# Last chunk's keys ahead of the last value projections, shifts stored by head group, rotary angles of self-attention computed in stage one, opening reordered

## The reference

```python
q = x @ W_q + b_q                      # x layer-normed, 512 rows
kv = y @ W_kv + b_kv                   # y: 8192 context rows
q, k = apply_rope(q, cos_q, sin_q), apply_rope(k, cos_k, sin_k)   # angle = position * frequency
attn = softmax(q @ k.T / sqrt(32))     # 16 heads of 32
x = x + (attn @ v) @ W_o + b_o
theta = pos * INV_FREQ * exp(log_scale)       # self-attention: one angle per head, row and pair
q, k = _rotate(q, cos(theta), sin(theta)), _rotate(k, cos(theta), sin(theta))
```

## Time and profile before

| | us |
|---|---|
| runs, median of 3 | 1724.97 (1720.51 to 1726.48) |
| profiled execution | 1718.63 |
| its span | 1717.3 |
| PE busy | 1598.6 (93%) |
| DVE busy | 1179.8 (69%) |
| ACT busy | 1080.9 (63%) |
| Pool busy | 720.7 (42%) |
| mean granted TensorE clock | 0.955 of full speed |

### The profile page before, as it was taken

How to read it: one execution, slowest core, us unless ns; L and a number is a source line. 1 busy time by engine, 2 the same in 40 slices (tenths; PEclk the granted TensorE clock), 3 DMA queues, 4 the chain that set the end, 5 groups by cost and what they waited for, 6 DMA issues and landing times.

```text
span 1717.3 us, 25439 instructions
## 1 busy us (share of the span) xinstructions
PE 1598.6 (93%) x9532; PEld 973.7 (57%) x9532; DVE 1179.8 (69%) x2759; ACT 1080.9 (63%) x1269; POOL 720.7 (42%) x385
## 2 busy tenths in 40 slices
PE   6599999999999779999999999999888879999998
PEld 4466666666666443434443444444655467888886
DVE  5567777777877759999988988998674452222222
...
GB/s 143 123 184 176 132 136 167 141 136 156 152 136 133 126 178 98 123 101 120 123 123 122 111 121 115 123 123 74 83 27 56 2 3 176 124 123 123 125 128 54
DMA packets 87339, 202.61 MB, mean 118 GB/s; under 512 B 8828, under 2 KB 9084, under 8 KB 84400
## 3 DMA queue, kind: packets, MB, share of 16 engines
...
## 4 chain that ended last, share of the span: by engine, by line
PE 77%; DVE 9%; issue 6%; ACT 5%; DMA 1%; POOL 1%; SPq 1%; DVEq 0%; ACTq 0%; POOLq 0%
PE PS L114 41%; PE PS L637 12%; PE PS L669 11%; PE PS L411 7%; DVE acc L660 2%; ACT P L643 2%; PE PS L679 1%; PE PS L828 1%; DVE rc L940 1%; PE PS L825 1%; DMA y<-in_wq 1%; DVE rel L424 1%; PE PS L153 1%; DVE rec L614 1%; PE PS L910 1%
## 5 line engine op out<-in xcount | busy, mean ns | idle before, releaser
L643 ACT ACTIVATE P<-PS 128x1024 f32<-128x1024 f32 x512 | 481.9, 1037 | 99.0 <-PE PS L637 81.7
L660 DVE TENSOR_TENSOR acc<-acc,P 128x2048 f32<-128x2048 f32 x216 | 507.7, 2414 | 34.3 <-ACT P L643 34.2
L424 DVE CUSTOM_DVE_ANT_0 rel<-PS,rel 128x256 f32<-128x256 f32 x1024 | 363.2, 420 | 135.8 <-PE PS L411 131.4
L417 ACT ACTIVATE rel<-PS 128x1024 f32<-128x1024 f32 x256 | 263.3, 1029 | 113.1 <-PE PS L411 109.2
L669 PE MATMUL PS<-P,qe 128*32 128x512 f32 x2048 | 258.8, 604 | 0.7 <-ACT on L674 0.7
L108 POOL TENSOR_TENSOR w3l<-qk,w3h 128x2048 fp32r<-128x2048 f32 x2 | 9.1, 4562 | 482.7 <-ACT w3h L105 482.7
L108 POOL TENSOR_TENSOR El<-We,Eh 128x1536 fp32r<-128x1536 f32 x36 | 126.0, 3501 | 166.3 <-ACT Eh L105 166.2
L114 PE MATMUL PS<-Wh,R 128*128 128x512 f32 x512 | 188.3, 424 | 0.0
L114 PE MATMUL PS<-R,Eh 128*128 128x512 f32 x576 | 182.2, 397 | 3.0 <-POOL El L108 3.0
L114 PE MATMUL PS<-R,Wh 128*128 128x512 f32 x512 | 167.3, 408 | 10.0 <-ACT kr L510 9.0
L411 PE MATMUL PS<-khd,qh 32*128 32x256 f32 x2048 | 134.0, 336 | 29.6 <-POOL khd L384 10.7
...
## 6 DMA issues: line engine op xcount, KB each, us to landing
khd<-kscr SPq DMA_DIRECT2D x129, 256.0 KB, 4.0
...
qe<-vscr SPq DMA_DIRECT2D x64, 256.0 KB, 4.7
kl<-kscr SPq DMA_DIRECT2D x63, 256.0 KB, 3.9
```

What stands on the lines that cost most here:

```text
L417: return AC.sig(nc.scalar.activation(rel[i][:, :, :, :], PS[:, 2 * b:2 * b + 2, :].rearrange("p j (t n) -> p j t n", t=2), ACT.Relu))
L424: m = DV.sig(nc.vector.tensor_tensor_reduce(out=rel[i][:, j, t, :], in0=PS[:, 2 * b + j, t * 256:(t + 1) * 256], in1=rel[i][:, j, t, :], s ...
L643: expm[s, pr] = spfree[b] = AC.sig(nc.scalar.activation(P[s % 4][:, 2 * pr:2 * pr + 2, :], PS[:, 2 * b:2 * b + 2, :], ACT.Exp, scale=SCALE))
L660: accm[s] = DV.sig(nc.vector.tensor_tensor(a[:, :, :], a[:, :, :], P[s % 4][:, :, :], ALU.add))
```

## The change

- The opening loads the first context chunk and the key weights first and warms PE with 40 instead of 22 transposes. The angles of the table come first on DVE, then the split of chunk 0; three key units run before the query input is transposed and a fourth before the queries are projected. The queries are swapped by a DVE shuffle and rotated group by group in slots of units 4 to 9 (`rotate_query`, `query_high`, `query_low`). The first chunk's ropes run on DVE. The low halves of `wq`, `wv` and chunk 0 are DVE's.
- Pairs start at slot 120 and follow every 11 slots until they are back in the old places at pair 48; from pair 112 on they follow every 10.
- In the last two chunks the order is keys of 14, keys of 15, values of 14, values of 15. The queries are loaded right behind the last unit.
- Shifts are reduced, transposed, copied and written to row 96 for each head group by itself (`maxima_out`, `maxima_rows`), and stage two waits for the group that it needs. `hot` puts a matmul in each third slot behind the last unit. The three rows of ones are set behind the barrier.
- The angles of self-attention are computed on DVE in 28 steps in units 29 to 56 (`angle_step`), their sines and cosines on ACT in units 64 to 75 (`wave_step`). `ks` and `vo` get tiles of their own, and `cs2` first serves as `ang` and `nn`.

```diff
+        t_ex = AC.sig(nc.scalar.activation(ex[:, :], cst[:, 4:8], ACT.Exp))
...
-        ks, vo = cs2[:, 0, :, :], [cs2[:, 1, :, :]]
+        ks, vo = sbx("ks", [128, 4, 512]), [sbx("vo", [128, 4, 512])]
         cs = [sbx(f"cs{i}", [128, 2, 512]) for i in range(2)]
-        ang = sbx("ang", [128, 1536])
-        nn = sbx("nn", [128, 1536])
+        ang, nn = [cs2[:, i, :, :].rearrange("p a b -> p (a b)")[:, 0:1536] for i in range(2)]
...
-        wq, wk, wv, xn, qsw = y[0], vo[0], kr[1], ks, ks
+        wq, wk, wv, xn, qsw = ks, vo[0], kr[1], qe, kr[1]
...
+        t_y0 = load_input(0)
         t_wk = lane("l_wk").dma(SP, wk[:, :, :], wkv_[:, :, 0:512])
+        t_x = l_a.dma(SP, X[:, :, :], A["x"].rearrange("o (t p) d -> p (o t) d", p=128))
+        t_wq = l_w.dma(SP, wq[:, :, :], A["wq"].rearrange("(k p) n -> p k n", p=128))
...
+        warm(40, 7)
...
+        t_y0s = split(y[0][:, :, :], yh[0][:, :, :], yl[0][:, :, :], t_y0)
+        SP.wait(t_y0s)
+        t_y1 = load_input(1)
+        t_wks = split(wk[:, :, :], Wh[:, :, 0:512], Wl[:, :, 0:512], t_wk)
...
+        t_cs = AC.sig(nc.scalar.mul(nn[:, 0:1024], sinv[:, 0:1024], -1.0))
+        SP.wait(t_cs)
+        for hf in range(2):
+            for s in range(2):
                 for t, src in ((0, cosv), (1, nn if s == 0 else sinv)):
-                    t_cscr = l_t.dma(SP, cscr[:, hf, s, :, t, :], src[:, hf * 512:(hf + 1) * 512])
+                    t_cscr = l_t[hf].dma(SP, cscr[:, hf, s, :, t, :], src[:, hf * 512:(hf + 1) * 512])
...
+        t_wqs = split(wq[:, :, :], wqh[:, :, :], wql[:, :, :], t_wq)
...
+        def rotate_query(g):
+            z, x_ = qsw[:, g, :], qe[:, g, :]
+            DV.wait(ev[g], ev_sign, t_wvs)
+            m_ = DV.sig(nc.vector.stream_shuffle(z, x_, halves))
+            DV.wait(m_)
+            a = DV.sig(nc.vector.tensor_tensor(x_, x_, cosq, ALU.mult))
+            b_ = DV.sig(nc.vector.tensor_tensor(z, z, sinq, ALU.mult))
+            DV.wait(a, b_)
+            qrot[g] = DV.sig(nc.vector.tensor_tensor(x_, x_, z, ALU.add))
+        def query_high(g):
+            AC.wait(qrot[g])
+            qhm[g] = AC.sig(nc.scalar.copy(qh[:, g, :], qe[:, g, :]))
+        def query_low():
+            DV.wait(qhm[3], qrot[3])
+            t_ql = DV.sig(nc.vector.tensor_tensor(ql[:, :, :], qe[:, :, :], qh[:, :, :].bitcast(F32), ALU.subtract))
+            SP.wait(qhm[3], t_ql)
+            qout.append(write_parts(SP, l_q, (qh, ql)))
...
+            DV.wait(kev[c][g], t_wqs, ropes.get((c - 1, g)))
             m = DV.sig(nc.vector.stream_shuffle(z, x, halves))
-            PL.wait(m, csm[c])
-            a = PL.sig(nc.gpsimd.tensor_tensor(x, x, ct[:, 0, :], ALU.mult))
-            b_ = PL.sig(nc.gpsimd.tensor_tensor(z, z, ct[:, 1, :], ALU.mult))
-            PL.wait(a, b_)
-            ropes[c, g] = PL.sig(nc.gpsimd.tensor_tensor(x, x, z, ALU.add))
-            PL.wait(ropes[c, g], max_last.get(c - 2))
-            khd_m[c, g] = PL.sig(nc.gpsimd.tensor_tensor(khd[c % 2][:, g, 512:768], x[:, 0:256], x[:, 256:512], ALU.subtract))
+            E = PL if c else DV
+            E.wait(m, csm[c])
+            a = E.sig(E.e.tensor_tensor(x, x, ct[:, 0, :], ALU.mult))
+            b_ = E.sig(E.e.tensor_tensor(z, z, ct[:, 1, :], ALU.mult))
+            E.wait(a, b_)
+            ropes[c, g] = E.sig(E.e.tensor_tensor(x, x, z, ALU.add))
+            E.wait(ropes[c, g], max_last.get(c - 2))
+            khd_m[c, g] = E.sig(E.e.tensor_tensor(khd[c % 2][:, g, 512:768], x[:, 0:256], x[:, 256:512], ALU.subtract))
...
+        angle_steps, trig, wave = [], [None] * 4, {}
+        def load_positions():
+            SP.wait(t_cscr, list(qrot.values()))
+            wave["pos"] = l_a.dma(SP, cosv[:, 0:512], A["c_pos"].to_broadcast([128, 512]))
+        def first_angle():
+            DV.wait(wave["pos"], t_ex)
+            wave["pr"] = DV.sig(nc.vector.tensor_scalar(cosv[:, 512:1024], cosv[:, 0:512], cst[:, 2:3], None, ALU.mult))
+        def angle_step(g, k):
+            a, n_ = cs2[:, 1, g, :], cs2[:, 0, g, :]
+            DV.wait(trig[g] if k else wave["pr"])
+            if k == 0:
+                ins = nc.vector.tensor_scalar(a, cosv[:, 512:1024], ex[:, g:g + 1], None, ALU.mult)
+            elif k == 1:
+                ins = nc.vector.tensor_scalar(n_, a, INV2PI, MAGIC, ALU.mult, ALU.add)
+            elif k == 2:
+                ins = nc.vector.tensor_scalar(n_, n_, MAGIC, None, ALU.subtract)
+            elif k < 6:
+                ins = nc.vector.scalar_tensor_tensor(a, n_, -(P2A, P2B, P2C)[k - 3], a, ALU.mult, ALU.add)
+            else:
+                ins = nc.vector.tensor_scalar(a, a, 3.1415925, -3.1415925, ALU.min, ALU.max)
+            trig[g] = DV.sig(ins)
+        def wave_step(g, k):
+            a, n_ = cs2[:, 1, g, :], cs2[:, 0, g, :]
+            AC.wait(wave[g, k - 1] if k else trig[g])
+            if k == 0:
+                ins = nc.scalar.activation(n_, a, ACT.Abs)
+            elif k == 1:
+                ins = nc.scalar.activation(a, a, ACT.Sin, scale=cst[:, 20:21])
+            else:
+                ins = nc.scalar.activation(n_, n_, ACT.Sin, scale=-1.0, bias=hpi[:, 0:1])
+            wave[g, k] = AC.sig(ins)
...
+        def hot(n):
+            for _ in range(n):
+                nc.tensor.matmul(PS[:, 7, :], qh[:, 0, 0:128], qh[:, 0, :], start=True, stop=True)
...
+        def maxima_out(g):
+            DV.wait(DV.last())
+            t_nmg[g] = DV.sig(nc.vector.tensor_reduce(nm[:, g:16:4, :], mpart[:, g:16:4, :, :], AX, ALU.max, negate=True))
+        def maxima_rows(g):
+            PE.wait(t_nmg[g], bank[1][0], nm_free.get(g - 1))
+            for qt in range(4):
+                ins = nc.tensor.transpose(PS[0:4, 6, qt * 128:(qt + 1) * 128], nm[:, g:16:4, qt], ident[:, :])
+            AC.wait(PE.sig(ins))
+            nm_free[g] = m = AC.sig(nc.scalar.copy(nmT[32 * g:32 * g + 4, :], PS[0:4, 6, :]))
+            SP.wait(m, k_use[NCH - 1], k_use[NCH - 2])
+            for j, x_ in enumerate((Wh, Wl)):
+                t_qmx[g] = l_nm[g].dma(SP, x_[96:97, :, :].rearrange("p a b -> p (a b)")
+                                       .rearrange("p (h g n) -> p h g n", h=2, g=4)[:, :, g, :],
+                                       nmT[32 * g + 2 * j:32 * g + 2 * j + 2, :])
...
+        def first_key(c):
+            return 8 * c - (4 if c == NCH - 1 else 0)
+        for g, u in enumerate((4, 5, 7, 9)):
+            at(u, 0, rope, 0, g)
+            at(u, 1, rotate_query, g)
+            at(u + 1, 4, key_high, 0, g)
+            at(u + 1, 8, query_high, g)
+        at(12, 0, query_low)
+        at(26, 0, load_positions)
+        at(28, 0, first_angle)
+        for g in range(4):
+            for k in range(7):
+                at(29 + 7 * g + k, 0, angle_step, g, k)
+            for k in range(3):
+                at(64 + 3 * g + k, 11, wave_step, g, k)
         for c in range(NCH):
             if c + 1 < NCH:
+                d = 0 if c else 4
                 for k, (u, m) in enumerate(((0, 9), (1, 4), (1, 9), (2, 4))):
-                    at(8 * c + u, m, y_high, c + 1, k)
-                at(8 * c + 2, 4, y_low, c + 1)
+                    at(8 * c + u + d, m - (7 if c == 14 else 0), y_high, c + 1, k)
+                at(8 * c + 2 + d, 4 - (7 if c == 14 else 0), y_low, c + 1)
             for g in range(4):
-                at(8 * c + g + 1, 10, rope, c, g)
-                at(8 * c + g + 5, 4, key_high, c, g)
-            at(8 * c + 8, 5, key_low, c)
+                if c:
+                    at(first_key(c) + g + 1, 10, rope, c, g)
+                    at(first_key(c) + g + 5, 4, key_high, c, g)
+            at(first_key(c) + (8 if c else 11), 5, key_low, c)
             for i in range(8):
-                at(8 * c + 6 + i, 2, maxima_1, c, i)
-                at(8 * c + 6 + i, 7, maxima_2, c, i)
-        for c in range(NCH):
-            kev[c] = []
-            for u in range(8):
+                n = 8 * c + i
+                m = max(12 * (6 + n), 12 * 10 + 11 * n) - 2 * max(0, n - 8 * 14)
+                at_slot(m + 2, maxima_1, c, i)
+                at_slot(m + 7, maxima_2, c, i)
+                if c == NCH - 1 and i % 2:
+                    at_slot(m + 9, maxima_out, i // 2)
+                    at_slot(m + 17, maxima_rows, i // 2)
+        order = [(c, u) for c in range(NCH - 2) for u in range(8)]
+        order += [(NCH - 2 + v % 2, 4 * h + u) for h in range(2) for v in range(2) for u in range(4)]
+        for c, u in order:
+            kev.setdefault(c, [])
+            if True:
+                if c == 0 and u == 3:
+                    query_input()
+                if c == 0 and u == 4:
+                    k_use[-1] = project_queries()
+                    maxfree[0], maxfree[2] = ev[3], ev[1]
+                    t_wvs = split(wv[:, :, :], Wh[:, :, 512:1024], Wl[:, :, 512:1024], t_wv)
+                    PE.wait(t_wvs)
...
-                if c == 0 and u == 3:
```

(37 more changed lines are left out.)

171 lines of the change are left out of this document (74 added, 97 removed).

## The result

The kernel got slower. Before took 1723.86 us (median of 18 runs, 1719.55 to 1730.62), after 1734.53 us (18 runs, 1724.29 to 1737.68); the ratio is 1.0048, with a 95% interval of 1.0035 to 1.0061, some 8.3 us, and the medians differ by 10.7. The profiled execution of after took 1726.68 us (span 1725.4), 8.05 more than that of before (1718.63), so the two traces hold nearly all of the difference. The forecast was 1718 with a range of 1699 to 1735: the range holds the time, the sign is wrong.

What follows compares the result with a forecast made beforehand. PE's own work was taken to bound stage one's middle, with stalls in the opening, at stage one's end and stage two's start. Terms -7.0 + 23.1 - 10.8 - 11.1 - 1 = -6.8 off the 1724.97 median gave 1718, range 1699 to 1735.

Steps and rivals of the forecast that it cites:

- opening: Start of stage one: 10.6 us of work done before the second pair, which comes 3.6 us later; -7.0 us.
- body without angles and waves: Middle of stage one: closer pairs +2 and +3.6, drifting casts and evacuations +1.5, waits in the last chunks +3.
- angle steps, wave steps: Body of stage one: 28 angle steps on DVE cost +10.5 us, 12 wave steps and a table load on ACT +2.5.
- end of stage one, start of stage two: Last projection to first score: 40.0 us becomes 26.5, with 2.7 us of pairs moved into the body; -10.8 us.
- stage two: Accumulations no longer slowed by Pool's angle work, 2.287 us against 2.945 each; -11.1 us.
- self-attention: ACT passes and a table load leave, but the w3h cast still waits for its weights; -1 us.
- 28 steps are 3.5 chunks: +10.5: Body of stage one: DVE angle steps wait for Pool and delay the maxima passes, 3.0 us a chunk; +10.5 us.
- less 0.2 of PE's own slack for each late one: In the angle-step sum: PE absorbs 0.2 us of each late pass, turning 4.3 us a chunk into 3.0.
- Rival 2: Body of stage one: Pool locks DVE, mean loss 1.0 us a step, 28 us in all, kernel 1735; chance 0.20.
- upper bound of 28 us: Angle steps in stage one: 28 x 1.0 us if the 11-slot stretch takes away DVE's gaps.
- Rival 1: Body of stage one: angle steps fit in DVE's gaps, body +8 instead of +23, kernel 1703; chance 0.27.
- Rival 3: Opening gives nothing back: loads land later or PE is cold through the query projection; kernel 1725; chance 0.11.

Runs made afterwards that it cites:

- noang: The changed kernel without the 28 angle steps, the position load and the 12 wave steps; 1714.61 us, ratio to before 0.9931.
- after_again: The changed kernel, unchanged, profiled a second time; 1735.07 us (one run).
- shuf: The changed kernel with each of the 28 angle steps replaced by a stream shuffle of the same size; 1714.87 us, ratio to before 0.9953.
- best: The changed kernel with angles on GpSimd in stage one, early key-tile loads, wv split before query projection, 26 self-attention fillers; 1689.68 us, ratio to before 0.9800.

## Why the prediction was wrong

By its own terms, in us, measured from the two profiled traces (the angles by after against noang):

| term | forecast | measured |
|---|---|---|
| opening | -7.0 | -8.2 |
| body without angles and waves | +10.1 | +11.2 |
| angle steps, wave steps | +13.0 | +20.4 |
| end of stage one, start of stage two | -10.8 | -8.2 |
| stage two | -11.1 | -9.2 |
| self-attention | -1.0 | +2.1 |
| sum | -6.8 | +8.1 |

(Opening: 10.6 of work done, 94.46 less 92.03 late. Body: 609.9 less 583.8 is 26.1; less the opening and the 2.7 of two pairs is 31.6, of which 20.4 are noang's. End: 29.1 less 40.0 is -10.9, plus 2.7. The last two: 574.2 less 583.4; 1224.59 less 1216.65, less all above, and 0.1 behind it.)

- **The step that failed** is "28 steps are 3.5 chunks: +10.5", 0.4 us of PE a step. The mechanism was the one of the earlier trace rows, and the trace shows it: instructions that end with GpSimd's. The size was wrong: 18.2 us with the first product, 0.63 an instruction. By PE's idle and busy time in chunks 3 to 6 of after, less noang's, the 7.7 us too many have three parts (rounded):
  - 4.3 us are the granted clock, at half for some 10 us in all behind stalls of 1.85 to 2.85 us. The sum had no term for what a stall does to the clock.
  - 1.8 us are PE's wait for `first_angle` in chunk 3. The sum priced the 28 steps and not this product.
  - The waits for the steps are 12.0 us in place of 10.5. The count of phases gave 4.3 a chunk, and chunks 4, 5 and 6 had waits of 3.6, 4.4 and 4.0: the count was near, although the single steps met other GpSimd instructions than it said. What failed in it is "less 0.2 of PE's own slack for each late one", which made 3.0 of the 4.3.
  In all, chunks 3 to 6 lost 3.2, 3.7, 5.8 and 5.5. The excess of the steps' durations on DVE is 18.8 us; that this is close to 18.2 is chance, since only 13.9 of it reached PE as waits.
- **Rival 2** ("Pool locks DVE", 1735) shares its mechanism with the forecast and priced it at 1.0 a step, with the point of decision at 0.8; 0.63 was measured, so it did not come true either. That its 1735 is so near the median of 1734.53 is luck: the other half of the miss is spread, 2.6 in the tail, 1.9 in stage two, 3.1 in self-attention, and most of after's runs are of the long kind (after_again), which puts the median 8 us above the profiled run.
- What the Trainium skill says under "Who interferes with whom" (SBUF — State Buffer) agrees with the trace as to which instructions wait: the two-input form with up to 4.02 us and the tensor-scalar form with up to 3.72 do, and shuf's single-input shuffle, 0.80 us at most, does not. The upper bound of 28 us, which the prediction called nearer by that rule, was not reached: 11 of the 29 met no running GpSimd instruction that held them up.
- **Rival 1** ("the steps fit") is refuted by the 94 instructions that PE lost from 200 to 320 us; shuf shows that the gap in DVE's time would have held them at little cost. **Rival 3** falls: the opening gave 8.2.
- **Opening**: right in each step (second pair, DVE's chain, 5 us of PE idle). But the 5 us idle were taken as the price of the wv split. The price was that the whole DVE chain started 11 us late (61.71, and 50.55 in best).
- **Waves** cost 3.9 in after and 2.3 to 2.4 in five other traces, forecast 2.5. **Pairs at 11 and 10 slots, drift, last chunks**: 11.2 against 10.1. The stall forecast at the last `key_high` was 0.9 us, at 593.88, and not 3. Instead chunks 1 and 2 took 71.4 us where before's took 64.6, and 4.3 of this are waits of PE, the longest (1.86 us, to 104.27) while GpSimd's chain was late (the product of 3.28 us in the chain above).
- **End**: forecast 26.5 from the last block to the first score, measured 29.1. The load of the first key tile, behind the shift rows on SyncE's queue, was left out, and made the first score 1.2 us later than the rows of ones alone would have; the clock fell to half at 619, which the prediction had left open at +3. The Exp's table load, 1.28 us, is behind it on the path.
- **Self-attention**: the weights' load, issued only behind the barrier, took 8.0 us for its first part in after and 5.8 in before, and the ScalarE passes that left had been cover, not cost. The first figure is partly luck: in five other traces with the same load it was 6.3 to 7.6.
- The stated tests: "accumulations at 2.29" came true (2.30), as did the second pair; the first score at 638.93 was 1.1 us short of the 640 that would have spoken for rival 2, and stage two gained 9.2, over the 8 below which the prediction would have failed. The tests did not catch the wrong sign.
